# Loading the next step's weights ahead of the gathered rows, and the padding rows inside the seventh step, in a routed-experts stage on one core

## Chip, core and metric

The kernel runs on one NeuronCore of a Trainium2 chip, in float32 throughout. The metric is device time in microseconds of one execution. Engines are named as in the profile: PE (TensorE), PEld (its weight loads), DVE (VectorE), ACT (ScalarE), POOL (GpSimd) and SP (SyncE, which here only issues DMAs; SPq is its queue).

## The reference

The input is a batch of B = 4 images of C = 256 channels and T = 1024 tokens. Three layers follow one another, each on the output of the one before:

```python
x = conv_attention(x)          # group norm, q/k/v, softmax(q k), output projection, + normed x
t = tokens(x)                  # (4, 1024, 256)
t = t + attention(ln(t))       # q, k, v each by x + silu(x W1) W2, then a softmax over queries
xf = layernorm(ln(t))          # routed experts: E = 8, top 2
probs = softmax(xf @ gate_w)
dispatch_w, expert_idx = top_k(probs, 2)
for e in range(8):
    h = gelu(xf @ w1[e] + b1[e])        # w1[e]: 256 x 1024
    y = h @ w2[e] + b2[e]               # w2[e]: 1024 x 256
    out = out + combine[:, e] * y
t = t + ln(t) + out
```

## The kernel before

Images 0 to 3 go through both attention layers one after another (`image(b)` on each engine). The rows of an image that the experts need are scattered by POOL into the DRAM table `sorted_rows`, grouped by expert (`send_rows`). The residual rows `r_out` are made by ACT (`stream`) and stored by SP into the DRAM table `acc_rows` (`rows_of`), on which POOL later adds the experts' weighted outputs.

The experts' stage works in steps of 256 rows (`STEP`) that belong to one expert. There are at most 40 steps, 36 of them live with these inputs (numbers 0 to 35). Steps 0 to 9 are written out, two at a time (`for i in range(LOOP_AT)`), because the rest of the last image's work (its gate, ranks, step tables, residual rows and its rows for the experts) is woven into them by tables such as `STREAM_AT` and `ROWS_AT`. Their rows come from the images before. Steps 10 to 35 run in a loop over pairs of steps (`Fori(LOOP_AT, PAIRS)`), which reads its expert, first row, and whether the expert's weights are new (`fresh`) from small tables in SBUF.

What a step s does:

- SP gathers its 256 rows (`gather`, `xg<-sorted_rows`) and, where the step is fresh, loads the raw weights `w1r` and `w2r` (1 MB each, `weights`), and always the biases (`biases`). Weights, rows and biases have two buffers each, by the parity n of the step.
- ACT and DVE split the raw weights of step s into a high and a low float32r part, in eight pieces (`w_piece`: ACT line 955, then DVE line 1512). They do it one piece after each chunk of the step before, s - 1: the first piece stands in ACT's order behind the gelu of chunk 0 of step s - 1, ahead of the gelu of chunk 1.
- PE turns the rows (`x_turn`, line 1910) in step s - 1 at its chunk 1. Then it makes the products (line 1645): per chunk f of eight, a first product `ps<-xt,w1s` (six matmuls), three chunks ahead, and a second product `ps<-w2s,hs` (six matmuls) that waits for DVE's split of the gelu output (`hs`, lines 1608 and 1610).
- DVE adds the bias of step s at chunk 1 of step s + 1 (`y_bias`, line 1554). ACT scales at chunk 3 of step s + 1 (`y_scale`, line 1034). POOL then adds the rows to `acc_rows` by two indirect DMAs (`scatter`, line 751), waits for them, and notes the row numbers and weights of a later step (`note_step`, lines 741 and 742, semaphore `noted`).

SP's order is one queue. In its iteration s, written `expert_load(s, ...)` and then `gather(s + 2, ...)`, it waits for the split of older weights, issues the weights of s if fresh, waits for `y_dve` (the bias add of step s - 2), issues the biases of s, waits for `noted` of step s (at the end of POOL's work in step s - 1), and gathers the rows of s + 2. After iteration 9 it stores the last residual rows, writes nine blocks of padding rows into `sorted_rows` behind each expert's rows, waits for them, and enters the loop:

```python
for i in range(LOOP_AT):
    steps(i, i == 0)
rows_of(B - 1)
```

Of the kernel before, what the change touches and what calls it, by code (L numbers as in the profile page):

```python
# [29 lines left out]
P = 128  # L30
# [15 lines left out]
def at(turn, per_turn, n):  # L46

    return turn * per_turn + n

def hybrid_block_kernel(nc, x, q_w, k_w, v_w, oT, q_b, v_b, out_b, gn, W1, W2T, a_qk, a_vT, Wout,
                        gate_w, w1, b1, w2, b2, ln_g, ln_b, out):
    B, C, T = x.shape
# [6 lines left out]
    E = gate_w.shape[1]  # L60
# [3 lines left out]
    STEP = 256  # L64
    SUB = STEP // P
# [5 lines left out]
    ROW = C + 16  # L71
    WEIGHT, NUMBER = C, C + E
    PAD = E * CAP
# [9 lines left out]
    sorted_d = nc.dram_tensor("sorted_rows", (PAD + STEP, ROW), F32, kind="Internal").ap()  # L83
# [5 lines left out]
    with ctx:  # L89
# [341 lines left out]
        WEIGH_AT = (4, 7)  # L431
        TABLE_AT = {(5, 1): 0, (5, 3): 1, (5, 5): 2}
        ROWS_AT = {5: (0, 1), 6: (2, 3), 7: (4, 5), 8: (6, 7)}
        STREAM_AT = {(5, 1): 0, (5, 5): 1, (6, 1): 2, (6, 5): 3, (7, 1): 4, (7, 5): 5, (8, 1): 6, (8, 5): 7}

        FOLDS = (SQ, VO, VA, QA, KA, VB)
# [24 lines left out]
        def _(sp):  # L462
# [33 lines left out]
            def rows_of(b):  # L496

                sp.wait_ge(r_ready, at(b, NT, NT))
                sp.sem_inc(sp_held, 1)
                sp.dma_start(acc_t[:, bass.ds(b * NT, NT), :], r_out[:, :, :]).then_inc(tok_out, 16)  # L500
# [11 lines left out]
            def weights(n, e):  # L512
                sp.dma_start(w1r[:, n, :].rearrange("p (k f) -> p k f", k=KC),
                             w1_d[bass.ds(e, 1)].rearrange("e p k f -> (e p) k f")).then_inc(w1_in[n], 16)
                sp.dma_start(w2r[:, n, :].rearrange("p (f c) -> p f c", f=FC),
                             w2_d[bass.ds(e, 1)].rearrange("e p f c -> (e p) f c")).then_inc(w2_in[n], 16)

            def no_weights(n, u):
                sp.wait_ge(w1_in[n], at(u, 16, 0))
                sp.sem_inc(w1_in[n], 16)  # L520
                sp.wait_ge(w2_in[n], at(u, 16, 0))
                sp.sem_inc(w2_in[n], 16)

            def biases(n, e):
                sp.dma_start(b1t[:, n, :], b1[bass.ds(e, 1)].rearrange("e p f -> (e p) f")
                             ).then_inc(b_in[n], 16)
                sp.dma_start(b2t[:, n, :], b2[bass.ds(e, 1), :].to_broadcast((P, C))).then_inc(b_in[n], 16)

            def gather(s, n, first):
                if not first:  # L530
                    sp.wait_ge(xt_mm, at(s, 1, -1))
                    sp.sem_inc(sp_held, 1)
                    sp.wait_ge(noted, at(s, 2, -2))
                    sp.sem_inc(sp_held, 1)
                row = sp.value_load(row_of[0:1, bass.ds(s, 1)], min_val=0, max_val=PAD)  # L535
                sp.dma_start(xg[:, n, :, :], sorted_d[bass.ds(row, STEP), :].rearrange("(h p) c -> p h c", p=P)
                             ).then_inc(g_in[n], 16)

            def expert(s):
                return sp.value_load(expert_of[0:1, bass.ds(s, 1)], min_val=0, max_val=E - 1)  # L540

            def expert_load(s, n, u):

                sp.wait_ge(ws_act, at(s, 8, -8))
                sp.sem_inc(sp_held, 1)
                sp.wait_ge(ws_dve, at(s, 8, -8))
                sp.sem_inc(sp_held, 1)
                e = expert(s)
                with sp.If(sp.value_load(fresh[0:1, bass.ds(s, 1)], min_val=0, max_val=1) == 1):  # L549
                    weights(n, e)  # L550
                with sp.Else():
                    no_weights(n, u)
                sp.wait_ge(h_act, at(s, FC, -FC))
                sp.sem_inc(sp_held, 1)
                sp.wait_ge(y_dve, at(s, 1, -1))
                sp.sem_inc(sp_held, 1)
                biases(n, e)

            weights(0, expert(0))
            biases(0, expert(0))  # L560
# [3 lines left out]
            weights(1, expert(1))  # L564
            biases(1, expert(1))

            def steps(i, first):
                for n in range(2):
                    s = i * 2 + n
                    if not first:  # L570
                        expert_load(s, n, i)
                    gather(s + 2, n, False)

            for i in range(LOOP_AT):
                steps(i, i == 0)
            rows_of(B - 1)

            sp.wait_ge(tab_b, 1)
            sp.wait_ge(pad_made, 2)  # L580
            for e in range(E + 1):
                at_row = sp.value_load(pad_at[0:1, e:e + 1], min_val=0, max_val=PAD - STEP) if e < E else PAD
                sp.dma_start(sorted_d[bass.ds(at_row, STEP), :].rearrange("(h p) c -> p h c", p=P),
                             pad_row[:, :].unsqueeze(1).to_broadcast((P, SUB, ROW))).then_inc(pad_in, 16)
            sp.wait_ge(pad_in, (E + 1) * 16)
            sp.wait_ge(rows_in, B * NT * 2 * 16)
            with sp.Fori(LOOP_AT, PAIRS) as i:
                with is_live(sp, i):
                    steps(i, False)

            s_end = final_step(sp)
# [2 lines left out]
            for n in range(2):  # L595

                sp.wait_ge(g_in[n], at(s_end, 8, 24))
                sp.sem_inc(sp_held, 1)
            sp.wait_ge(tok_out, (B + 1) * 16)
            ends(sp, 1, (pe_end, act_end, dve_end))  # L600
            for g in range(G):
# [1484 lines left out]
```

## Time and profile before

| | us |
|---|---|
| median of 3 runs (1392.93 to 1395.61) | 1393.78 |
| the profiled execution: its time | 1394.08 |
| its span, first to last instruction | 1392.4 |
| PE busy | 1176.3 (84%) |
| DVE busy | 805.4 (58%) |
| ACT busy | 573.0 (41%) |
| POOL busy | 293.3 (21%) |
| mean granted clock of TensorE | 0.929 |

The experts' stage begins about 703 us into the span and its last step ends at about 1350 us; 43 us of output follow. A row of the timeline gives start, duration, engine, line, operation, output and inputs, how many instructions are merged, and in brackets how long the engine stood idle before it and which work ended that. The granted clock is a share of full speed: 1.00 is 2.4 GHz, and an engine at the lower of its two levels runs at 1.2 GHz. An x_turn of step s + 1 stands in the middle of step s, so the distance from one x_turn to the next is the length of a step.

### The profile page before, as it was taken

What the parts mean: (1) busy time and instruction counts of PE and PEld (TensorE: products, weight loads), DVE (VectorE), ACT (ScalarE), POOL (GpSimd) and SP (SyncE); (2) the same over time, 40 slices, a digit from 0 to 9 for tenths busy, and PEclk for the clock granted to TensorE, in tenths of its full rate; (3) what the DMA queues carried; (4) which work ended last, traced back from release to release, by engine and by line L of the source; (5) the groups of instructions that cost most, each with busy time, mean ns of one, the idle gap of its engine ahead of it and who ended that gap; (6) DMA issues with size and microseconds to landing.
All of it is one profiled execution on the core that took longest, in us unless ns stands there. A gap on an engine that the chain in (4) does not pass through costs nothing. (4 is left out here: it accounts for less than half of the span.)

```text
span 1392.4 us, 24905 instructions
## 1 busy us (share of the span) xinstructions
PE 1176.3 (84%) x8066; PEld 1097.9 (79%) x8067; DVE 805.4 (58%) x1915; ACT 573.0 (41%) x1042; POOL 293.3 (21%) x323
## 2 busy tenths in 40 slices
PE   6999999999999999999976877455776675699993
PEld 5898998889898898989876867455775575599992
DVE  4674566656666566664676556254655465475651
ACT  3432535325353254532445545243434344354431
POOL 2010003005040050400433123321222121133330
PEclk9999999999999999999998998878897887899997
DMA  4000000001000010000425254555345435423337
GB/s 148 1 31 1 1 0 32 31 1 65 3 31 31 1 65 1 31 1 5 149 77 143 40 152 129 162 149 144 98 103 146 144 97 147 138 54 58 58 54 246
DMA packets 82147, 103.35 MB, mean 74 GB/s; under 512 B 11792, under 2 KB 71312, under 8 KB 82064
## 3 DMA queue, kind: packets, MB, share of 16 engines
q1 hardware_dynamic: 68624, 84.96, 19.3%
q0 software_dynamic: 13440, 17.32, 7.1%
q8 instruction: 48, 0.79, 0.2%
q14 instruction: 35, 0.29, 0.1%
HBM read 74.05 MB, written 29.25 MB: 74 GB/s over the span
## 5 line engine op out<-in xcount | busy, mean ns | idle before, releaser
L1645 PE MATMUL ps<-w2s,hs 128*128 128x256 f32 x1728 | 274.2, 298 | 168.7 <-DVE hs L1610 168.4
L1645 PEld LDWEIGHTS ps<-w2s,hs 128*128 128x128 f32 x1728 | 243.6, 206 | 176.1 <-DVE hs L1610 174.7
L1645 PE MATMUL ps<-xt,w1s 128*128 128x256 f32 x1746 | 271.4, 294 | 0.0
L1645 PEld LDWEIGHTS ps<-xt,w1s 128*128 128x128 f32 x1746 | 241.7, 202 | 0.0
L751 POOL DMA_INDIRECT acc_rows<-y_w,now_s x72 | 120.6, 1675 | 361.8 <-ACT y_w L1034 220.7
L1016 ACT ACTIVATE h<-ps,b1t 128x256 f32<-128x256 f32 x288 | 137.1, 478 | 99.0 <-PE ps L1645 79.5
L1512 DVE TENSOR_TENSOR w1s<-w1r,w1s 128x512 fp32r<-128x512 f32 x88 | 60.1, 685 | 184.4 <-ACT w1s L955 184.4
L955 ACT CAST w1s<-w1r 128x512 fp32r<-128x512 f32 x100 | 61.5, 617 | 236.2 <-DMA w1r<-in_w 221.2
L1610 DVE TENSOR_TENSOR hs<-h,hs 128x256 fp32r<-128x256 f32 x288 | 127.7, 444 | 9.9
L1608 DVE CAST hs<-h 128x256 fp32r<-128x256 f32 x288 | 91.2, 317 | 66.4 <-ACT h L1016 38.2
L1645 PE MATMUL ps<-xs,wh 128*128 128x512 f32 x384 | 121.1, 397 | 1.6 <-issue 1.6
L1645 PEld LDWEIGHTS ps<-vk,pr 128*128 128x128 f32 x768 | 95.9, 190 | 4.5 <-DVE pr L1466 2.3
L1645 PE MATMUL ps<-vk,pr 128*128 128x256 f32 x768 | 97.1, 282 | 1.8 <-DVE pr L1466 1.8
L673 POOL DMA_INDIRECT sorted_rows<-xf,slot_i x64 | 69.7, 1090 | 134.0 <-ACT prob L902 100.6
L1645 PE MATMUL ps<-vs,pr 128*128 128x256 f32 x768 | 97.7, 282 | 0.0
L1645 PE MATMUL ps<-xs,qs 128*128 128x512 f32 x384 | 95.3, 397 | 0.0
L1645 PE MATMUL ps<-qs,ks 128*128 128x512 f32 x384 | 92.0, 390 | 0.0
L1645 PEld LDWEIGHTS ps<-vs,pr 128*128 128x128 f32 x768 | 91.9, 188 | 0.0
L1645 PEld LDWEIGHTS ps<-xs,wh 128*128 128x128 f32 x384 | 69.4, 188 | 14.5 <-issue 1.8
L1645 PEld LDWEIGHTS ps<-qs,ks 128*128 128x128 f32 x384 | 70.1, 188 | 13.2
L1645 PEld LDWEIGHTS ps<-xs,qs 128*128 128x128 f32 x384 | 69.8, 188 | 13.4
L1461 DVE TENSOR_REDUCE neg_max<-ps 128x1 f32<-128x1024 f32 x32 | 39.2, 1224 | 68.6 <-PE ps L1645 68.6
(232 smaller groups left out, 1805.0 us busy)
## 6 DMA issues: line engine op xcount, KB each, us to landing
w1r<-in_w SPq DMA_DIRECT2D x22, 1024.0 KB, 5.0
w2r<-in_w SPq DMA_DIRECT2D x22, 1024.0 KB, 7.5
xg<-sorted_rows SPq DMA_DIRECT2D x38, 272.0 KB, 2.8
b2t<-in_b SPq DMA_DIRECT2D x36, 128.0 KB, 3.0
xn<-in_x SPq DMA_DIRECT2D x4, 1024.0 KB, 4.9
acc_rows<-r_out SPq DMA_DIRECT2D x4, 1024.0 KB, 4.9
rows<-acc_rows SPq DMA_DIRECT2D x8, 512.0 KB, 7.3
out_tokens<-cols_out SPq DMA_DIRECT2D x8, 512.0 KB, 8.9
```

The lines of the kernel that those rows point to most:

```text
L673: g.indirect_dma_start(out=sorted_d, out_offset=bass.IndirectOffsetOnAxis(ap=slot_i[:, k, t:t + 1], axis=0), in_=xf[:, t, :], in_offset=No ...
L751: g.indirect_dma_start(out=acc_d, out_offset=bass.IndirectOffsetOnAxis(ap=now_s[:, n, h:h + 1], axis=0), in_=y_w[:, n, h, :], in_offset=No ...
L955: a.copy(hi[:, c], (w1r, w2r)[f // 4][:, n, c]).then_inc(ws_act, 1)
L1016: a.activation(h32[:, gi % 4, :], bank(gi % 4, STEP), ACT.Gelu, bias=b1t[:, n, f:f + 1]).then_inc(h_act, 1)
L1461: v.tensor_reduce(neg_max[:, i:i + 1], bank(2 * (i % 2), count=2), AXX, ALU.max, negate=True).then_inc(s2_max, 1)
L1512: v.tensor_tensor(lo[:, c], (w1r, w2r)[f // 4][:, n, c], hi[:, c].bitcast(F32), ALU.subtract).then_inc(ws_dve, 1)
L1608: v.tensor_copy(hs[0][:, f, :], h32[:, gi % 4, :]).then_inc(h_hi, 1)
L1610: v.tensor_tensor(hs[1][:, f, :], h32[:, gi % 4, :], hs[0][:, f, :].bitcast(F32), ALU.subtract).then_inc(h_lo, 1)
L1645: ins = t.matmul(out, left[l], right[r], start=first and n == 0, stop=last and n == 2, **more)
```

## The change

SP's iteration s now issues three things in another order, and for another step: `load_weights(s + 1)`, `gather(s + 2)`, `load_biases(s + 1)`. The load of the expert's number stands inside, behind the waits. Iteration 0 has only the gather. The padding rows are written in iteration 6, and the last residual rows in iteration 8, for which ACT's eight `stream` pieces move six to nine chunks earlier (`STREAM_AT`). At the end SP waits for one more pair of biases, which the last iteration loads without use.

```diff
-        STREAM_AT = {(5, 1): 0, (5, 5): 1, (6, 1): 2, (6, 5): 3, (7, 1): 4, (7, 5): 5, (8, 1): 6, (8, 5): 7}
+        STREAM_AT = {(4, 0): 0, (4, 7): 1, (5, 1): 2, (5, 5): 3, (6, 1): 4, (6, 5): 5, (7, 1): 6, (7, 5): 7}
...
-            def expert_load(s, n, u):
+            def load_weights(s, n, u):
 
                 sp.wait_ge(ws_act, at(s, 8, -8))
                 sp.sem_inc(sp_held, 1)
                 sp.wait_ge(ws_dve, at(s, 8, -8))
                 sp.sem_inc(sp_held, 1)
-                e = expert(s)
                 with sp.If(sp.value_load(fresh[0:1, bass.ds(s, 1)], min_val=0, max_val=1) == 1):
-                    weights(n, e)
+                    weights(n, expert(s))
                 with sp.Else():
                     no_weights(n, u)
+
+            def load_biases(s, n):
                 sp.wait_ge(h_act, at(s, FC, -FC))
                 sp.sem_inc(sp_held, 1)
                 sp.wait_ge(y_dve, at(s, 1, -1))
                 sp.sem_inc(sp_held, 1)
-                biases(n, e)
+                biases(n, expert(s))
...
-            def steps(i, first):
+            def steps(i):
                 for n in range(2):
                     s = i * 2 + n
-                    if not first:
-                        expert_load(s, n, i)
+                    begin = isinstance(i, int) and s == 0
+                    if not begin:
+                        load_weights(s + 1, 1 - n, (i if n == 0 else i + 1))
                     gather(s + 2, n, False)
+                    if not begin:
+                        load_biases(s + 1, 1 - n)
+                    if isinstance(i, int):
+                        if s == 6:
+                            write_pads()
+                        if s == 8:
+                            rows_of(B - 1)
+
+            def write_pads():
+
+                sp.wait_ge(tab_b, 1)
+                sp.wait_ge(pad_made, 2)
+                for e in range(E + 1):
+                    at_row = sp.value_load(pad_at[0:1, e:e + 1], min_val=0, max_val=PAD - STEP) if e < E else PAD
+                    sp.dma_start(sorted_d[bass.ds(at_row, STEP), :].rearrange("(h p) c -> p h c", p=P),
+                                 pad_row[:, :].unsqueeze(1).to_broadcast((P, SUB, ROW))).then_inc(pad_in, 16)
...
+            sp.wait_ge(b_in[0], at(s_end, 16, 48))
+            sp.sem_inc(sp_held, 1)
```

How SP's queue reads in the program for the second half of a pass of the loop, where `w1r`, `w2r` are the raw weights, `b1t`, `b2t` the biases and `xg` the gathered rows. Before:

```order
L513 DMA w1r<-in_w 128x2x1024
L515 DMA w2r<-in_w 128x8x256
...
L525 DMA b1t<-in_b 128x8
L527 ISA
L527 DMA b2t<-in_b 128x256
L533 ISA
L535 ISA
L535 TENSOR_LOAD row_of
L535 ISA x2
L536 ISA
L536 DMA xg<-sorted_rows 128x2x272
```

And the same half pass in the change:

```order
L513 DMA w1r<-in_w 128x2x1024
L515 DMA w2r<-in_w 128x8x256
...
L535 TENSOR_LOAD row_of
L535 ISA x2
L536 ISA
L536 DMA xg<-sorted_rows 128x2x272
L540 REGISTER_ALU
L540 TENSOR_LOAD expert_of
L540 ISA x2
L525 ISA
L525 DMA b1t<-in_b 128x8
```

The gather, with its wait, has moved behind the weights and ahead of the biases, and a load of `expert_of` now stands between the waits and the biases. The weights are those of the step after.

SP's queue where it leaves the written-out steps and enters the loop, before: the last gather of iteration 9, the residual rows, the padding rows (the first of nine), and the loop.

```order
L536 DMA xg<-sorted_rows 128x2x272
L500 DMA acc_rows<-r_out 128x8x256
L582 TENSOR_LOAD pad_at
L582 ISA x2
L583 ISA
L583 DMA sorted_rows<-pad_row 128x2x272
...
L583 DMA sorted_rows<-pad_row 128x2x272 x2
L587 UNCONDITIONAL_BRANCH
L587 ISA
L448 TENSOR_LOAD live
```

The padding rows in the change, between the biases of step 7 and the weights of step 8 (the last two of the nine, and what follows):

```order
L588 TENSOR_LOAD pad_at
L588 ISA x2
L589 ISA
L589 DMA sorted_rows<-pad_row 128x2x272 x2
L548 TENSOR_LOAD fresh
L548 ISA x2
L548 COMPARE_AND_BRANCH
L540 TENSOR_LOAD expert_of
L540 ISA x2
L513 ISA
L513 DMA w1r<-in_w 128x2x1024
```

The nine writes no longer stand between iteration 9 and the loop; they stand ahead of the weights of step 8, and the residual rows (not shown) stand ahead of the weights of step 10.

## Rows read from the trace of the kernel before

**Rows 1.** Busy time by stretch: two runs of fresh steps, then steps without new weights

```profile
924.08:1029.90 105.82, 68.75 (x503) 67.54 (x502) 58.59 (x134) 44.70 (x97) 19.36 (x20) 0.82 0.47 130
1041.52:1231.38 189.86, 123.67 (x903) 121.28 (x901) 104.38 (x238) 79.73 (x173) 34.86 (x36) 0.82 0.45 128
1231.38:1347.62 116.24, 116.24 (x1002) 116.24 (x1001) 70.13 (x182) 49.17 (x110) 36.73 (x40) 1.00 0.34 58
```

**Rows 2.** Who waited for whom, 924 to 1231 us

```profile
ACT w1s L955 <- DMA w1r<-in_w: 146.0, 14, 12.1
```

**Rows 3.** Timeline of SP's queue, 944 to 968 us

```profile
944.07 0.39 SPq L536 DMA_DIRECT2D xg<-sorted_rows  x1
947.45 0.38 SPq L513 DMA_DIRECT2D w1r<-in_w  x1
...
955.41 0.35 SPq L525 DMA_DIRECT2D b1t<-in_b  x1
...
966.04 0.39 SPq L536 DMA_DIRECT2D xg<-sorted_rows  x1
968.21 0.38 SPq L513 DMA_DIRECT2D w1r<-in_w  x1
```

**Rows 4.** Timeline of ACT in the same step

```profile
952.53 0.62 ACT L955 CAST w1s<-w1r 128x512 fp32r<-128x512 f32 x1 [12.09 <-DMA w1r<-in_w]
```

**Rows 5.** Timeline of PE, 925 to 960 us: the second products it waited for

```profile
932.51 1.65 PE L1645 MATMUL ps<-w2s,hs 128*128 128x256 f32 x6 [7.13 <-DVE hs L1610]
...
954.59 1.65 PE L1645 MATMUL ps<-w2s,hs 128*128 128x256 f32 x6 [8.70 <-DVE hs L1610]
```

**Rows 6.** Timeline of DVE in the same step: the bias add

```profile
954.45 0.68 DVE L1554 TENSOR_TENSOR y_b<-ps,b2t 128x512 f32<-128x512 f32 x1
```

**Rows 7.** Timeline of POOL in the same step

```profile
957.94 1.75 POOL L751 DMA_INDIRECT acc_rows<-y_w,now_s  x1 [14.73 <-ACT y_w L1034]
```

**Rows 8.** DMA issues over the whole span: last number, median us to landing

```profile
sorted_rows<-xf,slot_i POOLq DMA_INDIRECT x64, 2.8
```

**Rows 9.** DMA issues from 826 to 832 us only: KB each, us to landing

```profile
w1r<-in_w SPq DMA_DIRECT2D x1, 1024.0 KB, 6.7
...
sorted_rows<-xf,slot_i POOLq DMA_INDIRECT x4, 6.3
```

**Rows 10.** DMA issues from 847 to 854 us only

```profile
w1r<-in_w SPq DMA_DIRECT2D x1, 1024.0 KB, 5.6
...
sorted_rows<-xf,slot_i POOLq DMA_INDIRECT x4, 5.2
```

**Rows 11.** Timeline of PE, 755 to 925 us: stalls of steps 2 to 9

```profile
759.40 0.97 PE L1645 MATMUL ps<-w2s,hs 128*128 128x256 f32 x6 [2.87 <-DVE hs L1610]
...
774.23 1.06 PE L1983 MATMUL ps<-gate_sb,xfT 128*128 128x8 f32 x8 [3.95 <-ACT xfT L975]
...
815.35 1.65 PE L1645 MATMUL ps<-w2s,hs 128*128 128x256 f32 x6 [4.93 <-DVE hs L1610]
...
837.27 1.65 PE L1645 MATMUL ps<-w2s,hs 128*128 128x256 f32 x6 [4.11 <-DVE hs L1610]
...
858.59 1.65 PE L1645 MATMUL ps<-w2s,hs 128*128 128x256 f32 x6 [8.10 <-DVE hs L1610]
...
875.07 0.97 PE L1645 MATMUL ps<-w2s,hs 128*128 128x256 f32 x6 [2.11 <-DVE hs L1610]
...
912.00 1.65 PE L1645 MATMUL ps<-w2s,hs 128*128 128x256 f32 x6 [24.84 <-DVE hs L1610]
```

**Rows 12.** Timeline of SP's queue, 886 to 905 us

```profile
887.41 0.41 SPq L500 DMA_DIRECT2D acc_rows<-r_out  x1
888.65 11.45 SPq L583 DMA_DIRECT2D sorted_rows<-pad_row  x9
904.81 0.40 SPq L513 DMA_DIRECT2D w1r<-in_w  x1
```

**Rows 13.** Busy time by stretch: step 5

```profile
809.00:832.00 23.00, 14.92 (x105) 13.81 (x104) 16.21 (x53) 9.73 (x21) 7.83 (x8) 0.85 0.57 152
```

More of the change, by code:

```diff
@@ L565, in _ @@
             biases(1, expert(1))
-            def steps(i, first):
+            def steps(i):
                 for n in range(2):
                     s = i * 2 + n
-                    if not first:
-                        expert_load(s, n, i)
+                    begin = isinstance(i, int) and s == 0
+                    if not begin:
+                        load_weights(s + 1, 1 - n, (i if n == 0 else i + 1))
                     gather(s + 2, n, False)
-            for i in range(LOOP_AT):
[L575 to L584, printed above, removed]
+                    if not begin:
[12 more added lines that the diff above has]
+                                 pad_row[:, :].unsqueeze(1).to_broadcast((P, SUB, ROW))).then_inc(pad_in, 16)
+            for i in range(LOOP_AT):
+                steps(i)
             sp.wait_ge(pad_in, (E + 1) * 16)
@@ L588, in _ @@
                 with is_live(sp, i):
-                    steps(i, False)
+                    steps(i)
             s_end = final_step(sp)
```

## The prediction

> **What bounds the kernel now.** I read the busy time by stretch first, since the experts' stage mixes two kinds of steps. Ten steps without new weights take 116.24 us, so 11.62 each, with PE busy all the time at the full clock [rows 1]. Fourteen fresh steps take 105.82 and 189.86 us, so 21.1 each, and there no engine is full: PE is busy 65%, at a granted clock of 0.82 [rows 1]. The waits say why: ACT waited 14 times, 146 us in all, for the raw weights to land [rows 2]. ACT's first piece stands ahead of the gelu of chunk 1, so PE stalls at its second product of chunk 1 (8.70 us in one step) and restarts at half speed: 1.65 us for six matmuls [rows 5], where 0.97 us is the row after a short stall [rows 11]. That costs 2.1 us a step: PE is busy 123.67 / 9 = 13.7 us in a fresh step against 11.62 in the others [rows 1].
>
> I call that restart R. At R = 954.59 [rows 5] the loop of causes closes as follows. The bias add ends at 955.13, R + 0.54 [rows 6]; POOL starts the scatter at R + 3.35 [rows 7]; its landing frees the note, and SP gathers at 966.04, R + 11.45 [rows 3]. Only then does SP reach the next weights: 1.78 us after the gather's end (966.43 to 968.21) inside a pair of steps, 2.99 us (944.46 to 947.45) across the loop's end [rows 3]. The first cast starts 5.08 us after the issue at 947.45 [rows 3, 4], and PE restarts 2.06 us after that [rows 4, 5]. The sum is 11.45 + 0.39 + 1.78 + 5.08 + 2.06 = 20.8 us, or 22.0 across the loop's end; the mean is 21.4, and 21.1 is measured. So the length of a fresh step is set by this ring through POOL and the weights' landing, not by an engine.
>
> **The change, part by part.** Weights leave for step s + 2 in SP's iteration s + 1, right behind iteration s. Two rings remain, and I work out the length D of a fresh step from each.
>
> Ring A, over the bias add. Iteration s ends with the biases of s + 1, which wait for the bias add, R + 0.54. The issue came 0.28 us after it (955.13 to 955.41) [rows 3, 6]. Now the expert's number is loaded behind the wait. Nine padding writes with eight such loads took 11.45 us, 1.3 us for each pair, of which an issue is about 0.4 [rows 12]; I take 0.9 for the load. The two bias issues take 0.9 more, so they end at R + 2.6. The weights follow by 1.78 or 2.99 at R + 4.4 or R + 5.6, and with 5.08 + 2.06 the next restart is at 11.5 or 12.7. PE's own 11.62 is the floor of the shorter one, so the mean is 12.2. DVE comes to about the same: it is busy 104.38 / 9 = 11.6 us in a fresh step [rows 1], before any gap at a branch.
>
> Ring B, over POOL, spans two steps. The gather of iteration s + 1 stands ahead of its biases and waits for the note at R + 11.45. From its start to the end of the biases are 0.39 + 0.28 + 0.9 + 0.9 = 2.5 us, then 2.99 to the weights (the worse parity repeats), 5.08 and 2.06: 24.0 us for two steps, 12.0 each.
>
> Both rings rest on transfers that met empty queues. Now the weights fly from R + 4.4 to past R + 12, and POOL's scatter from R + 3.35 to R + 10 lies right inside. The trace before never has this pair together, so I bound it. From below, nothing is added. From above, I take row scatters of the last image with weights in flight. At 828 us the scatter landed in 6.3 us against 2.8 usual, and `w1r` in 6.7 against 5.1; at 850 us in 5.2 and 5.6 [rows 3, 4, 8 to 10]. Four scatters ran there, and now it is two, so I take the milder: 2.4 us on the note, 0.6 on the weights. Ring A becomes 12.8, ring B 12.0 + (2.4 + 0.6) / 2 = 13.5. With the harder pair (3.5 and 1.7) ring B gives 14.6. I take D = 13.5, with 12.2 and 14.6 as ends. The stall is then some 2 us, and the rows after 2.11 and 2.87 us restart at 0.97, those after 4.11 us and more at 1.65 [rows 11]. So I expect the full clock.
>
> Loop: 14 fresh steps, two of them the first of a run, where only ring A at 12.6 acts. After: 12 x 13.5 + 2 x 12.6 = 187; before 296; saved 109 us. The 10 and more steps without new weights stay at PE's 11.62.
>
> Steps 5 to 9, counted from restarts. Before, R5 to R10 is 815.35 to 932.51, 117.2 us, and the 4.93 us stall ahead of R5 goes as well [rows 5, 11].
> - R5 to R6: DVE has the step tables on top, 16.2 us busy [rows 13], so about 17.
> - R6 to R7: the padding. It starts when the biases of 7 are out, R6 + 2.6, with 0.9 for its first load and 11.45 for the nine [rows 12]. Queued behind it are the weights of 8, then the gather of 9 and the biases of 8. They leave at R6 + 2.6 + 0.9 + 11.45 + 1.8 = 16.8, land 5.1 later, and R7 is at R6 + 24. It was 21.3 (837.27 to 858.59) [rows 11]. So this step loses 2.7 us: the late weights move from step 9 to step 7.
> - R7 to R8: no fresh weights, the 2.11 us stall gone [rows 11], a cold restart of 2.1 on top of 11.6: 13.8 with rounding.
> - R8 to R9: the 1 MB of residual rows leaves about 2 us ahead of the weights of 10 and holds them some 3 us: R8 + 5.5 + 5.1 + 3 + 2.1 = 15.7. It was 36.9, with the 24.84 us stall [rows 11].
> - R9 to R10: ring A, and some slow clock: 13.
>
> Sum 83.5, so 33.7 + 4.9 = 38.6 saved; step 9 to 10 is also in the loop's 14, where it was given about 7, so 31.5 counts here.
>
> Steps 1 to 4: the weights of 3 move from behind POOL's note to behind the bias add, and the 2.87 and 3.95 us stalls go (ACT sat behind SP's count for a step without load) [rows 11], with some slow clock: 8. Weights of 2 move ahead of one gather only: 1. Small stalls of steps 3 and 4: an estimate of 1.5. Together 10.5. ACT's earlier `stream` pieces cost nothing: ACT is busy about 8.9 us of a fresh step (79.73 / 9) [rows 1], PE 11.62. The added wait at the end is for a transfer long landed, at most 0.5 us.
>
> Total: 109 + 31.5 + 10.5 = 151 saved from 1394.08, the profiled execution's own time (0.3 above the median): 1243.
>
> **The rivals.**
> - Contention is small (chance 0.25): the scatter and the weights share the engines with little loss, D = 12.2 to 12.6, and 12 steps give back 1.1 us each: 1230 and below to 1215 if the early steps are better too. For it: 256 rows of 1 KB are small beside 2 MB. Against: rows 9 and 10.
> - Contention is large (0.21): the note slips by 4 us or more, D = 15: 12 x 1.5 more, 1261. If the stall passes 4 us PE also restarts at half speed, 2.1 us a step: 1287. For it: a scatter that adds reads and writes, the row scatters only write. The Trainium skill, TensorE: Matmul & The Clock Gate, "HAM oscillation", says that a PE which waits for a transfer in every turn runs the next turn cold; before, the granted 0.82 agrees [rows 1].
> - Slower than before (0.02): the same mechanism, scatter behind weights, would have to eat the whole 151 us, D = 13.5 + 151 / 12 = 26, thus a note and weights late by 28 us together. It decides only from there; the longest slips in the rows are 3.5 and 1.7 us. Time 1400 and more.
> - No change (0.01): SP still reaches the weights only after POOL's note, as before. Then D stays 21 and the time is about 1394. The order of the queue speaks against it.
>
> **How the numbers follow.** The forecast, 1234 to 1256, has 0.51; the rivals have 0.25, 0.21, 0.02 and 0.01. Range 1220 to 1266: it holds the forecast's own range, most of the case of small contention and the milder half of the large. By over 0.2% (about what the runs can tell from no change) it is faster with 0.97, same 0.01, slower 0.02.
>
> **What would show it.** In the changed profile: ACT's wait for `w1r` falls from 146 us to below 40 in the loop; x_turn to x_turn is about 13.5 in fresh steps; `w1r` lands in 5.5 to 6 and `acc_rows` some 2 us later than before; PE's granted clock is near 1.00 in the loop; one stall of 10 us or more in step 7 and a small one in step 9. I am wrong if fresh steps are at 12 (no contention), if they are at 15 or cold, or if DVE turns out to be the bound with no wait for weights at all.

## The result, and the profile after

The change takes 1250.99 us (median of 4 runs, 1249.22 to 1254.58), and the kernel before took 1394.69 us beside it. The ratio is 0.897, with an interval from 0.8945 to 0.8999: 144 us saved by the medians, 10%. The profiled execution took 1252.58 us, of which 1250.7 are its span; the forecast was 1243.

The page of the changed kernel, busy time by engine and one group of instructions (busy time, mean ns of one, then idle time ahead of them and what ended it):

```profile
PE 1151.1 (92%) x8066; PEld 1069.8 (86%) x8067; DVE 806.2 (64%) x1915; ACT 572.7 (46%) x1042; POOL 296.1 (24%) x323
...
L966 ACT CAST w1s<-w1r 128x512 fp32r<-128x512 f32 x100 | 61.5, 617 | 74.5 <-DMA w1r<-in_w 71.2
```

PE lost 25 us of busy time (1176.3 before) without losing an instruction: those are products that no longer run at the lower clock. Busy time by stretch, with x_turns as the bounds (start and end, length, then busy time of PE, PEld, DVE, ACT, POOL, the granted clock, the DMA share and GB/s). The first row is the length from the x_turn in step 1 to the one in step 2; the last three answer to [rows 1]:

```profile
730.76:754.35 23.59, 15.69 (x111) 15.19 (x110) 18.13 (x32) 13.65 (x29) 10.13 (x7) 0.78 0.67 216
...
877.27:954.79 77.52, 63.39 (x503) 61.84 (x501) 58.70 (x135) 44.53 (x97) 21.05 (x22) 0.93 0.61 177
966.43:1090.77 124.34, 111.65 (x903) 107.80 (x902) 103.21 (x235) 76.93 (x170) 34.90 (x38) 0.99 0.64 182
1090.77:1207.02 116.25, 116.25 (x1003) 116.25 (x1002) 70.66 (x183) 49.57 (x110) 36.55 (x40) 1.00 0.34 58
```

The same fourteen fresh steps take 77.52 + 124.34 = 201.9 us, 14.4 each, where they took 295.7. In the second run of nine PE is busy 90% at a clock of 0.99, against 65% at 0.82. The ten steps without new weights are what they were (116.25). Laid against [rows 1], the fresh steps of the loop saved 28.3 + 65.5 = 93.8 us. From the x_turn that stands in step 1 to the one in step 5 the length fell from 79.8 (729.31 to 809.12) to 65.1 (730.76 to 795.87), 14.7 saved; from there to the one in step 10 from 115.0 to 81.4 (795.87 to 877.27), 33.6 saved. What lies ahead of and behind these bounds moved by under 0.5 us in sum.

The waits of the changed kernel from 877 to 1091 us (us in total, times, longest), the answer to [rows 2]:

```profile
POOL now_s L752 <- DMA acc_rows<-y_w,now_s: 79.6, 16, 7.4
...
ACT w1s L966 <- DMA w1r<-in_w: 46.6, 13, 8.7
...
PE ps L1656 <- DVE hs L1621: 26.8, 22, 6.5
```

The same view of SP's own waits in the nine fresh steps alone, 966 to 1091 us:

```profile
SPq L534 <- POOL now_w L753: 59.1, 10, 8.4
SPq L557 <- DVE y_b L1565: 8.9, 3, 4.9
```

SP waited ten times for POOL's note ahead of a gather, and three times for the bias add ahead of the biases.

ACT's wait for the weights fell from 146.0 to 46.6 us in all fourteen fresh steps. On top now stands a wait that was short before: POOL's for its own scatter. Its timeline shows which part of it is new (in brackets the idle time and what ended it):

```profile
1023.12 0.26 POOL L752 CAST now_s<-xg 128x2 int32<-128x2 f32 x1 [6.13 <-DMA acc_rows<-y_w,now_s]
...
1036.87 0.19 POOL L752 CAST now_s<-xg 128x2 int32<-128x2 f32 x1 [6.42 <-DMA acc_rows<-y_w,now_s]
...
1045.97 0.19 POOL L752 CAST now_s<-xg 128x2 int32<-128x2 f32 x1 [3.22 <-DMA acc_rows<-y_w,now_s]
```

And this is the same place in the kernel before:

```profile
964.85 0.19 POOL L741 CAST now_s<-xg 128x2 int32<-128x2 f32 x1 [3.19 <-DMA acc_rows<-y_w,now_s]
```

Either the scatter meets the weights and POOL waits 5.9 to 7.4 us, or it doesn't, and it waits 2.0 to 3.6 us. In the second run of fresh steps it is 7 of 10 times the long wait, in both together 9 of 16. Laid beside SP's queue, each of the nine long waits belongs to a second scatter that was issued between 1.3 us after and 1.2 us before a `w1r` load; where the load left 2.0 us later or more, or there was none, the wait was short.

### The profile page after: what moved, and what is told of

Same layout as the page of the kernel before. It is cut to its first block and busy times, and to the rows that moved or that the text cites. A ratio compares the mean times of both kernels' runs of the same rounds, so it can differ in the third digit from the quotient of the medians.

```text
span 1250.7 us, 24975 instructions
## 1 busy us (share of the span) xinstructions
PE 1151.1 (92%) x8066; PEld 1069.8 (86%) x8067; DVE 806.2 (64%) x1915; ACT 572.7 (46%) x1042; POOL 296.1 (24%) x323
## 5 line engine op out<-in xcount | busy, mean ns | idle before, releaser
L1656 PE MATMUL ps<-w2s,hs 128*128 128x256 f32 x1728 | 258.9, 285 | 54.9 <-DVE hs L1621 54.1
L1656 PEld LDWEIGHTS ps<-w2s,hs 128*128 128x128 f32 x1728 | 227.1, 192 | 63.8 <-DVE hs L1621 50.9
L1656 PE MATMUL ps<-xt,w1s 128*128 128x256 f32 x1746 | 260.4, 286 | 1.3 <-issue 1.2
L1656 PEld LDWEIGHTS ps<-xt,w1s 128*128 128x128 f32 x1746 | 229.4, 192 | 2.6 <-issue 2.2
L1656 PEld LDWEIGHTS ps<-xs,wh 128*128 128x128 f32 x384 | 69.4, 188 | 14.4 <-issue 1.8
```

What stands on the lines that cost most here:

```text
L1656: ins = t.matmul(out, left[l], right[r], start=first and n == 0, stop=last and n == 2, **more)
```

## The ring that is left, read from one timeline

The timeline of the changed kernel, all engines, from one bias add to the next but one (the rows of the ring alone):

```profile
1023.24 0.68 DVE L1565 TENSOR_TENSOR y_b<-ps,b2t 128x512 f32<-128x512 f32 x1
...
1026.74 1.74 POOL L762 DMA_INDIRECT acc_rows<-y_w,now_s  x1 [3.24 <-ACT y_w L1045]
...
1028.45 0.38 SPq L513 DMA_DIRECT2D w1r<-in_w  x1
1028.78 1.67 POOL L762 DMA_INDIRECT acc_rows<-y_w,now_s  x1 [0.30 <-issue]
...
1038.06 0.38 SPq L536 DMA_DIRECT2D xg<-sorted_rows  x1
...
1043.70 0.39 SPq L513 DMA_DIRECT2D w1r<-in_w  x1
...
1049.88 0.62 ACT L966 CAST w1s<-w1r 128x512 fp32r<-128x512 f32 x1 [5.09 <-DMA w1r<-in_w]
...
1051.80 0.68 DVE L1565 TENSOR_TENSOR y_b<-ps,b2t 128x512 f32<-128x512 f32 x1
```

This is the ring that the prediction calls B, by a lap of it that is a little longer than the mean: the nine fresh steps take 13.8 us each on average (124.34 / 9), the two of this lap 14.3. I lay it link by link beside what the prediction's numbers give, from bias add to bias add, which is the same length as from restart to restart:

| link | forecast | measured |
|---|---|---|
| bias add to POOL's scatter | 3.49 (954.45 to 957.94) | 3.50 |
| scatter to gather | 8.10 + 2.4 | 11.32, so 8.10 + 3.2 |
| gather to weights | 2.5 + 2.99 | 5.64 |
| weights to first cast | 5.08 + 0.6 | 6.18, so 5.08 + 1.1 |
| first cast to bias add | 1.92 (952.53 to 954.45) | 1.92 |
| two steps | 27.0 | 28.56 |

So the ring has the links that were forecast, and three of five have their lengths to within 0.15 us. The two that ride on transfers are 1.3 us too long: the scatter slipped by 3.2 us and not 2.4, the weights by 1.1 and not 0.6. The chain of waits, from 1019 to 1052 us, is the same ring, with its longest piece the scatter's transfer:

```profile
1028.78 7.21 DMA acc_rows<-y_w,now_s
```

Two more places of the changed kernel matter. PE's timeline, its restarts after a stall of over 3 us from step 1 on:

```profile
736.19 1.65 PE L1656 MATMUL ps<-w2s,hs 128*128 128x256 f32 x6 [4.12 <-DVE hs L1621]
...
742.89 1.65 PE L1656 MATMUL ps<-w2s,hs 128*128 128x256 f32 x6 [3.78 <-DVE hs L1621]
...
836.31 1.65 PE L1656 MATMUL ps<-w2s,hs 128*128 128x256 f32 x6 [8.98 <-DVE hs L1621]
...
885.12 1.65 PE L1656 MATMUL ps<-w2s,hs 128*128 128x256 f32 x6 [6.54 <-DVE hs L1621]
```

And SP's queue around the loop's entry, the answer to [rows 12], and SP's only wait from 868 to 877 us:

```profile
829.61 0.09 SPq L513 DMA_DIRECT2D w1r<-in_w  x1
...
868.98 0.70 SPq L525 DMA_DIRECT2D b1t<-in_b  x1
869.71 0.34 SPq L527 DMA_DIRECT2D b2t<-in_b  x1
876.62 0.38 SPq L513 DMA_DIRECT2D w1r<-in_w  x1
```

```profile
SPq L595 <- DMA sorted_rows<-xf,slot_i: 3.4, 1, 3.4
```

The stall of 8.98 us is the padding's in step 7. The one of 6.54 us in step 10 I had not forecast. Between the end of the issue of the last biases (870.05) and the next weights (876.62), those of step 11, lie 6.6 us at the loop's entry. For 3.4 us of them SP waits for the row scatters of the last image (`rows_in`, line 595). The other 3.1 us are its loads and branch into the loop, about the 2.99 us that each turn of the loop has [rows 3]. Before the change that wait stood there too, but SP's last wait there was for the padding writes. The row scatters are late themselves: POOL issued them behind a scatter of the experts' rows that had taken 9.21 us to land, as the chain of waits has it:

```profile
855.25 9.21 DMA acc_rows<-y_w,now_s
```

## The experiments

Each is compared with the kernel before on the same chip. The change's ratio is 0.897 (0.8945 to 0.8999).

**The order of the queue alone.** The new order of `steps`, with the residual rows, the padding and `STREAM_AT` where they were.

```diff
-                    if isinstance(i, int):
-                        if s == 6:
-                            write_pads()
-                        if s == 8:
-                            rows_of(B - 1)
...
             for i in range(LOOP_AT):
                 steps(i)
+            rows_of(B - 1)
+            write_pads()
```

> The new order of SP's queue alone (weights of s+1, rows of s+2, biases of s+1); padding rows, residual rows and ACT's stream pieces stay where they were. If the order carries the gain: the loop is as in the changed kernel, the 9 us stall of step 7 is gone, but the nine padding writes stand ahead of the weights of step 11, so step 10 stalls some 5 us less than its 6.5 plus what step 7 gave; 1246 us (1238 to 1256). Rival, the moves carry a good part since the padding made the 24.8 us stall before: 1265 us or more.

Measured: 1255.04 us (1252.55 to 1258.27), ratio 0.8998 (0.8976 to 0.9019), beside 1396.51 for the kernel before. The 25 us stall at the loop's entry is back, in step 10 and shorter, PE's timeline:

```profile
883.43 1.65 PE L1653 MATMUL ps<-w2s,hs 128*128 128x256 f32 x6 [17.21 <-DVE hs L1618]
```

The order alone thus carries 141 of the 144 us by the medians, and the two intervals overlap. I had expected 1246 us. The 5 us that it was to be faster than the change did not come: its one large stall of 17.21 us is as long as the two of the change together (8.98 and 6.54).

**The moved padding and residual rows alone.** The old order of the queue, with the writes in iterations 6 and 8 and the new `STREAM_AT`.

> The moves alone: padding rows in iteration 6, residual rows in iteration 8, stream pieces earlier; SP's order as before. Theory of the order: the fresh steps stay at 21 us; the padding now delays the weights of step 7 by 12 us and the weights of step 10 leave some 8 us earlier (they still wait for the last rows of the table): 1398 us (1388 to 1404), so no gain. Rival, the moves carry a good part: 1375 us or less.

Measured: 1396.59 us (1394.83 to 1400.67), ratio 1.0002 (0.9989 to 1.0016): nothing. Busy time by stretch, fresh steps of the loop as in [rows 1]:

```profile
930.65:1036.71 106.06, 69.97 (x503) 68.86 (x501) 58.79 (x135) 44.70 (x97) 19.40 (x20) 0.82 0.47 129
1048.32:1238.00 189.68, 125.61 (x903) 123.59 (x902) 104.79 (x239) 79.72 (x173) 34.97 (x36) 0.82 0.46 128
```

And PE's two large stalls:

```profile
851.46 1.65 PE L1650 MATMUL ps<-w2s,hs 128*128 128x256 f32 x6 [14.11 <-DVE hs L1615]
...
918.14 1.65 PE L1650 MATMUL ps<-w2s,hs 128*128 128x256 f32 x6 [14.11 <-DVE hs L1615]
```

In the old order the moved writes only moved delays about. In the kernel before PE stalled for 4.11, 8.10 and 24.84 us in steps 6, 7 and 9, 37.1 us in all [rows 11]; here it is 14.11, 7.29 and 14.11 in the same steps, 35.5 us.

**The wait at the loop's entry moved behind the weights.** SP's steps 10 and 11 are written out, and its waits for the last rows and the padding stand right ahead of the gather of step 12, the first that may need them.

```diff
+                    if begin is False and isinstance(i, int) and s == A_STEPS - 2:
+                        sp.wait_ge(pad_in, (E + 1) * 16)
+                        sp.wait_ge(rows_in, B * NT * 2 * 16)
                     gather(s + 2, n, False)
...
-            for i in range(LOOP_AT):
+            for i in range(LOOP_AT + 1):
                 steps(i)
-            sp.wait_ge(pad_in, (E + 1) * 16)
-            sp.wait_ge(rows_in, B * NT * 2 * 16)
-            with sp.Fori(LOOP_AT, PAIRS) as i:
+            with sp.Fori(LOOP_AT + 1, PAIRS) as i:
```

> The changed kernel, but SP's pair of steps 10 and 11 is written out and the wait for the padding and the last image's rows stands ahead of the gather of step 12, so the weights of step 11 no longer stand behind it. Theory: the 6.5 us stall of step 10 and its cold restart (2.1) go: 1242 us (1238 to 1247). Rival, the stall of step 10 comes from the residual rows and the ring over POOL: 1249 to 1253, the weights of 11 still late.

Measured: 1249.11 us (1245.91 to 1249.76), ratio 0.894 (0.8919 to 0.8961), so some 2 us won by the medians and 4 by the ratios, and perhaps none, since the intervals overlap. PE's stall in step 10 is down from 6.54 us to 3.41, by as much as the wait that was moved. Its timeline shows the stalls of steps 9, 10 and 11:

```profile
861.07 1.65 PE L1657 MATMUL ps<-w2s,hs 128*128 128x256 f32 x6 [2.84 <-DVE hs L1622]
...
878.07 1.65 PE L1657 MATMUL ps<-w2s,hs 128*128 128x256 f32 x6 [3.41 <-DVE hs L1622]
...
894.52 1.39 PE L1657 MATMUL ps<-w2s,hs 128*128 128x256 f32 x6 [3.13 <-DVE hs L1622]
```

This was a miss, in two ways. The moved wait was only 3.4 of the 6.54 us. And I had counted the stall as a cost that ends with its cause: from the x_turn in step 10 to the next the length fell from 20.28 to 16.72 us, but the one behind it rose from 12.85 to 16.98. On a ring a step that comes early waits in the next lap, for POOL's note: behind the moved wait SP's only one from 875 to 892 us is for the note, 6.5 us.

**The padding spread over four iterations.**

```diff
-                        if s == 6:
-                            write_pads()
+                        if s in PADS_AT:
+                            write_pads(PADS_AT[s])
...
+            PADS_AT = {6: (0, 1), 7: (2, 3), 8: (4, 5), 9: (6, 7, 8)}
```

> The changed kernel, but the nine padding writes are spread over iterations 6 to 9 (2, 2, 2, 3). Theory: the weights of step 8 leave some 8.5 us earlier, the 9 us stall of step 7 shrinks to about 1 and its cold restart goes, the 2.8 us in iterations 7 and 8 are hidden: 1241 us (1236 to 1247). Rival, the padding's cost is bandwidth, not its place in the queue: 1249 to 1253.

Measured: 1248.12 us (1244.46 to 1251.49), ratio 0.8932 (0.8911 to 0.8953). That is outside the 1236 to 1247 that I expected, and within the intervals of the change. The stall of 8.98 us in step 7 has gone, but one as long has come in step 9, ahead of the one in step 10 that the change has too (6.54 there):

```profile
858.14 1.65 PE L1658 MATMUL ps<-w2s,hs 128*128 128x256 f32 x6 [8.84 <-DVE hs L1623]
...
879.34 1.65 PE L1658 MATMUL ps<-w2s,hs 128*128 128x256 f32 x6 [6.60 <-DVE hs L1623]
```

In the change step 9 had no such stall. The weights of step 10 now leave behind two paddings and the 1 MB of residual rows. Again a delay was moved and not removed, which is not what the rival said either: it had the padding's cost as bandwidth, whatever its place.

**The biases ahead of the gather.** Weights of s + 1, biases of s + 1, rows of s + 2: the gather is then inside the ring over the bias add.

```diff
-                    gather(s + 2, n, False)
                     if not begin:
                         load_biases(s + 1, 1 - n)
+                    gather(s + 2, n, False)
```

> The changed kernel with the biases of s+1 ahead of the gather of s+2 (weights, biases, gather). This cuts the ring over POOL's note, and makes the ring over the bias add longer by one gather (1.6 us) before each weight issue. Theory: that ring then gives 13.7 plus 1 for slower landing, 14.7 in all fresh steps against 14.4 now: 1256 us (1248 to 1264). Rival, only the note's ring matters and the other has slack: fresh steps 13, 1235.

Measured: 1258.15 us (1256.58 to 1259.17), ratio 0.9013 (0.8985 to 0.9042), beside 1397.0, as expected. It is 7 us slower than the change by the medians and 6 by the ratios, whose intervals just touch. The profiles agree with the sum: the nine fresh steps take 131.31 us (962.68 to 1093.99), 14.6 each, where the change has 13.8. So the ring over the bias add, with the gather in it, is no shorter than the one over the note.

**Half of the weights' bytes.** Only the first half of `w1` and of `w2` is loaded, so the output leaves the other weights out.

> The changed kernel, but each weight load after the first two steps' moves half of its bytes (half of w1 and half of w2; the rest of the raw tile keeps what it had, so the output leaves those weights out). Theory, fresh steps are set by the ring scatter, note, gather, biases, weights, each slowed by the other's bytes: the scatter's landing beside weights falls from 7.2 us to about 5.5, w1r lands in 3 instead of 5.3, fresh steps fall from 14.4 to DVE's and PE's 12.2: 1213 us (1205 to 1226). Rival, the ring is SP's and POOL's instruction time, bytes don't matter: 1245 or more.

**A scatter that overwrites.** POOL's scatter without `compute_op=ALU.add`, so the output leaves the sums out.

> The changed kernel, but POOL's scatter of the experts' rows overwrites instead of adding (so the output leaves the sums out): the same bytes written, none read. Theory, the scatter lands late because its packets take turns with the weights' on the same DMA engines: landing beside weights stays near 7 us, 1245 to 1253. Rival, it is the read and write back of an adding scatter that suffers: landing falls to 5 or less, fresh steps to about 13, 1232.

Measured: 1225.81 us (1224.12 to 1227.8), ratio 0.8783 (0.8753 to 0.8813) with half of the bytes, and 1230.66 us (1228.91 to 1231.33), ratio 0.881 (0.8782 to 0.8838) with the plain scatter, both beside 1397.0. Expected were 1213 (up to 1226) for the first, and 1245 to 1253 for the second, where the rival had 1232: my reading that the scatter's kind hardly matters fell. Busy time by stretch of the nine fresh steps, 12.6 us each with half the bytes:

```profile
948.22:1061.64 113.42, 108.16 (x902) 105.66 (x901) 102.17 (x234) 76.86 (x169) 35.90 (x38) 1.00 0.48 121
```

and 12.8 us each with the plain scatter:

```profile
954.66:1070.03 115.37, 108.64 (x903) 105.81 (x902) 101.23 (x237) 76.96 (x171) 26.52 (x38) 1.00 0.61 196
```

POOL's timeline of the kernel with half the bytes shows a long wait all the same, 5.83 us, for a scatter issued 0.2 us before the weights:

```profile
991.62 1.67 POOL L768 DMA_INDIRECT acc_rows<-y_w,now_s  x1 [0.30 <-issue]
999.12 0.19 POOL L758 CAST now_s<-xg 128x2 int32<-128x2 f32 x1 [5.83 <-DMA acc_rows<-y_w,now_s]
```

and that of the plain scatter shows where its gain comes from:

```profile
984.67 1.14 POOL L762 DMA_INDIRECT acc_rows<-y_w,now_s  x1 [6.50 <-ACT y_w L1045]
986.11 0.97 POOL L762 DMA_INDIRECT acc_rows<-y_w,now_s  x1 [0.30 <-issue]
993.22 0.18 POOL L752 CAST now_s<-xg 128x2 int32<-128x2 f32 x1 [6.13 <-DMA acc_rows<-y_w,now_s]
```

The two issues take 1.14 + 0.97 us there and 1.74 + 1.67 in the change, so the ring is 1.3 us shorter before a byte moves. The wait for the landing beside the weights is as long as ever: 6.13 against 6.42 us. Half the weights took 5.6 us to land in place of 8.5 (`w2r`, median, 985 to 1040 us), and yet the scatter beside them held POOL for 5.83 us. The bytes do matter where the scatter comes later: issued 1.3 us after the load it held POOL for 3.9 to 4.8 us with half the bytes (three times), and for 6.4 to 7.4 us in the change (three times).

**The load of the expert's number, in two places.** Ahead of the biases' waits but behind the gather, and ahead of the gather as well. Only the ring over the bias add gets shorter by the first, both by the second. The edit of the first:

```diff
             def load_biases(s, n):
+                e = expert(s)
                 sp.wait_ge(h_act, at(s, FC, -FC))
...
-                biases(n, expert(s))
+                biases(n, e)
```

> The change, with the load of the expert's number moved ahead of the two waits in front of the biases, but still behind the gather. If the loop is set by the ring over POOL's note (the gather waits for the note, the biases and the weights queue behind it), the number's load stays inside that ring and nothing is won there: only the few steps on the ring over the bias add get shorter by 0.9 us, so 1247 to 1251 us beside the change's 1251. Rival: the ring over the bias add sets the fresh steps; then 12 or more of them lose 0.9 us each, and the time is 1240 or less.

> The change, with the same load moved ahead of the gather and of its wait for POOL's note, so that it lies on neither ring. If the ring over the note sets the loop, it is 0.9 us shorter over two steps, 0.45 per fresh step: 12 times 0.45 is 5.4 us, and with the few others 1243 to 1247 us. Rival (ring over the bias add sets the loop): the same 1240 or less as with the load behind the gather, so no difference between the two kernels. If the load costs much less than the 0.9 us that I read from the padding rows, both kernels stay within 2 us of the change.

Measured: 1252.03 us (1248.7 to 1254.7), ratio 0.8952 (0.8931 to 0.8973) for the first, and 1249.6 us (1244.02 to 1253.21), ratio 0.8936 (0.8912 to 0.896) for the second, both beside 1397.49. The first shuts out its rival as it was priced: 1240 would be a ratio of 0.887. So the ring over the bias add doesn't set most of the fresh steps, and SP's waits say it more directly than the times: in the nine fresh steps of the first kernel it waited 70.6 us for the note and 0.2 us for the bias add. The second came out above the 1243 to 1247 that I expected. Its interval overlaps with those of the first and of the change, so what the load costs on the ring over the note cannot be told from the times. What the load costs is seen in SP's queue itself. With the load behind the gather (the first kernel):

```profile
1037.41 0.38 SPq L536 DMA_DIRECT2D xg<-sorted_rows  x1
1038.78 0.34 SPq L525 DMA_DIRECT2D b1t<-in_b  x1
```

With the load ahead of it (the second):

```profile
1036.20 0.38 SPq L536 DMA_DIRECT2D xg<-sorted_rows  x1
1036.93 0.35 SPq L525 DMA_DIRECT2D b1t<-in_b  x1
```

From issue to issue it is 1.37 and 0.73 us: the load costs 0.64 us on the path, not the 0.9 that I had read from the padding rows.

**Weights two steps ahead.** SP's iteration s issues the weights of s + 2, the biases of s + 1 and the rows of s + 2. The weights then leave more than a step before ACT's first cast, and neither ring passes through their landing.

```diff
-                    if not begin:
-                        load_weights(s + 1, 1 - n, (i if n == 0 else i + 1))
-                    gather(s + 2, n, False)
+                    load_weights(s + 2, n, i + 1)
                     if not begin:
                         load_biases(s + 1, 1 - n)
+                    gather(s + 2, n, False)
```

> The changed kernel with SP's iteration s written as weights of s+2, biases of s+1, rows of s+2. The weights then wait only for the split of the buffer's old content, and leave about 5 us earlier than now, ahead of the bias add and of POOL's note; padding and residual rows come behind them. Theory, both rings are cut: fresh steps at 12.2 (DVE), loop 31 us shorter, stalls of steps 1, 7 and 10 gone: 1196 us (1186 to 1214). Rival, the DMA engines' bandwidth sets the fresh steps (weights plus scatter plus rows in 13.9 us): 1235 or more.

Measured: 1208.93 us (1208.1 to 1209.42), ratio 0.8656 (0.8629 to 0.8684): 42 us below the change, and with its two variants below the best here. It is 13 us above the 1196 that I expected, within the range. The rival, bandwidth, is out: it had 1235 or more, and the same bytes pass in steps of 12.1 us. The nine fresh steps are at 12.1 us, 0.5 above PE's floor, by the busy time by stretch:

```profile
937.62:1046.52 108.90, 105.92 (x903) 104.97 (x901) 101.64 (x235) 76.77 (x169) 36.70 (x37) 1.00 0.67 195
```

In these nine steps ACT has no wait for `w1r` left, so the weights' landing is out of the lap, as meant. But POOL's waits for its scatter fell too, to 2.0 to 4.5 us (29.3 us in 9 waits, where the change has seven of ten at 5.9 to 6.5), since the weights now leave 5 us or more before or after each of the scatters. So this run took two things away at once, the landing and the meeting of scatter and weights, and it does not show how much each of them is worth. Two large stalls are left: 5.66 us in step 1, and 6.15 us where step 11 begins, behind the loop's entry, with ACT waiting for a bias:

```profile
873.85 0.47 ACT L1026 ACTIVATE h<-ps,b1t 128x256 f32<-128x256 f32 x1 [9.12 <-DMA b2t<-in_b]
```

**The same with the entry's wait moved, and with the padding spread too.** The first has the moved wait of the third experiment on top of the one before, the second the spread padding of the fourth as well.

> The order with weights two steps ahead (1208.9 us), with SP's steps 10 and 11 written out and its waits for the last row scatter and the padding moved from ahead of step 10 to directly ahead of the gather of step 12. If the 6.15 us stall of PE in step 10 (ACT 9.1 us behind the bias b2t) comes from these waits, it goes, and since no ring over POOL carries it on here most of it should stay won: 1203, range 1199 to 1207. Rival: as in the change itself, the gain is passed on to the stalls of the steps behind, and the time stays at 1207 to 1210.

> The same, with the padding rows also spread over iterations 6 to 9 in place of all nine in iteration 6. With the weights two steps ahead the 10 us of padding writes in iteration 6 delay the biases and weights only where the slack of one step is used up. Theory: the two-ahead order already hides them, so spreading wins nothing: within 3 us of the kernel without it. Rival: the padding still holds a load on the path, and spreading wins 3 to 8 us.

Measured: 1209.85 us (1205.04 to 1210.64), ratio 0.8643 (0.862 to 0.8667), and 1208.68 us (1207.4 to 1210.04), ratio 0.8649 (0.8628 to 0.867), beside 1397.49. Both stay where the two-ahead order alone was, so the rival of the first was right in its number, and the theory of the second. In the first, the length from the x_turn in step 10 to the one in step 11 fell from 18.7 to 14.3 us, but ACT's timeline shows a smaller wait in each of the three steps from there (the first and the third):

```profile
873.24 0.47 ACT L1027 ACTIVATE h<-ps,b1t 128x256 f32<-128x256 f32 x1 [3.96 <-DMA b2t<-in_b]
...
899.20 0.48 ACT L1027 ACTIVATE h<-ps,b1t 128x256 f32<-128x256 f32 x1 [3.96 <-DMA b2t<-in_b]
```

The biases now queue behind 2 MB of weights: `b2t` was issued at 864.63, 2.3 us behind their last issue, and ACT had it at 873.24, 8.6 us later, where a `b2t` takes 3.0 us to land in the kernel before (median). That is the next thing to take apart, by issuing the biases ahead of the weights; it wasn't tried.

## Why the prediction came out as it did

The forecast of 1243 us was 8 us, or 0.6%, below the median, and its main mechanism held: the order of SP's queue, with a ring over POOL's note and a scatter slowed by the weights as what is left. Part of the nearness is luck, since two errors of opposite sign met in the sum. By its own steps:

- **What bounded the kernel before: right.** A ring through POOL's note and the landing of the weights, not an engine. The new order of the queue alone brought 141 us; moving the writes without it brought none.
- **Ring B, 12.0 us plus contention, D = 13.5: right in its links, too small by 0.5 us.** The mis-sized term is "I take the milder". The scatter slipped by 3.2 us and the weights by 1.1 in the lap shown, where the milder pair has 2.4 and 0.6 and the harder 3.5 and 1.7. Measured are 28.56 / 2 = 14.3 there, 13.8 as the mean of the nine steps of the second run, and 14.4 as the mean of all fourteen. Without the step at the loop's entry (20.28 us from 877.27 to 897.55) the mean is (201.9 - 20.3) / 13 = 14.0, so this term cost 13 x 14.0 - (187 - 12.6) = 7 us.
- **Ring A is the shorter one: right for most steps.** Shortening it alone does nothing that can be told. But three of the nine pairs of biases in the second run still waited for the bias add, and the chain of waits passes over it once, between the weights of 973.58 and those of 987.67. Its load was costed at 0.9 us and is 0.64.
- **Fresh steps at full clock: right.** The granted clock is 0.99 in the second run; in the first, with the stall of 6.54 us, it is 0.93. PE's stalls in the second stay below 2.8 us, and the row of the longest is 0.98 us long, not 1.65. So the rival "contention is large" is out: neither PE cold in every turn nor steps of 15 us came.
- **R9 to R10 at 13: wrong, 20.6 us (864.57 to 885.12).** I followed the padding to its new place and forgot what stood behind it in the queue: the wait for `rows_in` at the loop's entry, exposed for 3.4 us once the padding is gone. That is under half of the 7.6 us. The biases ended 5.5 us after R9 and not 2.6, since the gather ahead of them waited for a note behind the scatter of 9.21 us; the way into the loop took 3.1 us, where a step inside a pair has 1.8; and the weights took 6.33 us to land and not 5.08. In the sum this step is the other 8 us of the loop's missing 15 (109 forecast, 93.8 measured). But it is not 8 us of time: with the wait moved, the kernel won 2 us by the medians and 4 by the ratios, inside their intervals, because the ring over the note closes in behind it.
- **R6 to R7 at 24: right**, 23.1 us (813.24 to 836.31), with the weights of step 8 issued at 829.61, 16.4 us after R6 where I had 16.8. **R5 to R6 at 17**: 16.2. **R7 to R8 at 13.8**: 14.0. **R8 to R9 at 15.7**: 14.2, so the 3 us that I gave to the residual rows ahead of the weights of 10 were too much; how long they held them isn't shown.
- **Steps 1 to 4, 10.5 saved: too small, 14.7.** The length from the x_turn in step 2 to the one in step 3 went from 24.0 (755.22 to 779.23) to 14.2 us (754.35 to 768.57), 9.8 in one step, where I had taken 8; the other three gave 4.9 and not 2.5.
- **The sum.** Forecast 109 + 31.5 + 10.5 = 151; measured 93.8 + 33.6 + 14.7 = 142.1, and 141.5 between the two profiled executions. An overshoot of 15 in the loop and a shortfall of 6 ahead of it partly cancelled, which is the luck in it.
- **The signs that it named.** ACT's wait for `w1r` was to fall below 40 us and is 46.6. The stall of step 7 was to be 10 us or more and is 8.98. The small stall foretold for step 9 isn't there; the unforetold one is in step 10. The clock near 1.00 came in the second run only. `w1r` lands in 5.2 us (median of 14, 877 to 1091 us), below the 5.5 to 6 foretold.

The rival of small contention is settled too. It held that the packets take turns and the scatter loses some 0.5 us. The slip of 3.2 us speaks against it. The Trainium skill, DMA: Bandwidth & Descriptors, section "Queues, rings and completion order", tells of engines that take turns between queues by packets; the estimate of 0.5 us that I set beside it, with no row or figure behind it, was six times too small here. What exactly holds the scatter stays open. With a plain write POOL's waits came at the same two lengths as in the change (2.0 to 3.4 us, or 6.1 to 6.4); with half the bytes there were lengths between, 3.9 to 5.4 us, and the longest was 6.25 us. What the change's trace does show is that the time between the issue of the weights and that of the scatter went with a long wait or a short one. With the plain scatter a load that left 0.6 us behind it no longer held it (2.93 us), where in the change one 1.2 us behind it did (5.92).

Open is also how much of the 20 us that the plain scatter won is its shorter issue (1.3 us over two steps, so some 8 us in 12 steps) and how much is that the scatter meets the weights less often (7 long waits of 15 in the fourteen fresh steps, 872 to 1071 us, against 9 of 16 in the change).

## What to carry to other kernels

When the steps of a pipeline are longer than any engine's work, follow one lap from a restart to the next and write down each link; the change to make is the one that takes the longest landing out of the lap, and loading two steps ahead rather than one took out 42 us more than this change did. Time won at one stall can be given back at the next lap unless the lap itself got shorter: with the wait at the loop's entry moved, one step became 3.6 us shorter and the next 4.1 us longer. Look also for what else the change brings together: here 9 of 16 scatters met the weights, which the old order had kept apart. When work leaves a queue, read what stood behind it: its cover goes with it.

## What was not expected of the hardware

- A scatter of 2 x 128 rows that adds into DRAM landed in 3.9 us (median of 30 issues) in the fresh steps of the kernel before, where it met no weights, and in 7.2 us in the lap shown, 0.3 us behind a 2 MB load. The wait went with the lag: issued from 1.3 us after to 1.2 us before such a load, it held POOL for 5.9 to 7.4 us; issued 2.0 us before it or earlier, for 3.0 to 3.6 us. The load itself slowed less: `w1r` from 5.0 to 5.2 us and `w2r` from 7.5 to 8.4 us (medians of 14).
- An indirect DMA that adds holds POOL for 1.67 us at its issue, one that overwrites for 1.09 us (medians of 72 each).
- The length of a stall alone doesn't tell whether PE restarts at half speed. After 2.87 us of it the six matmuls took 0.97 us in the kernel before [rows 11], and after 2.84 us 1.65 us with the entry's wait moved; 3.13 us was followed by 1.39. The prediction had drawn the line near 4 us.
